# One gathered tile of 24 replaced by ScalarE column copies in a graph network layer

## The reference

```python
h = relu(layernorm(x))
m_in = concatenate([h[src], edge_attr], axis=1)
messages = relu(m_in @ msg_w1 + msg_b1) @ msg_w2 + msg_b2
aggregated = segment_sum(messages, dst, 12500)
u = relu(concatenate([h, aggregated], axis=1) @ upd_w1 + upd_b1)
out = x + u @ upd_w2 + upd_b2
```

## Time and profile before

| | us |
|---|---|
| median of 3 runs | 4632.11 |
| lowest to highest | 4628.16 to 4644.86 |
| the profiled execution | 4667.21 |
| its span in the trace | 4665.5 |

### The profile page before, as it was taken

One profiled execution on the slowest core, in us unless ns is written; L12 is line 12 of the kernel. 1 busy time (PEld: TensorE's weight loads), 2 busy tenths in 40 slices (PEclk: granted clock), 3 DMA queues, 4 the chain that ended last, 5 costly groups with the idle time before them and its releaser, 6 DMA issues.

```text
span 4665.5 us, 32266 instructions
## 1 busy us (share of the span) xinstructions
PE 2529.9 (54%) x10696; PEld 2174.4 (47%) x10696; DVE 1923.7 (41%) x1990; ACT 129.8 (3%) x257; POOL 2961.3 (63%) x3133
## 2 busy tenths in 40 slices
PE   5666555555555555555555555555555555535455
PEld 4555444444444444444444444444444444435344
DVE  4556343343343343443443443443433433434344
ACT  3310000000000000000000000000000000000000
POOL 5565666666666666666666666666666666656565
PEclk7777666676676666666666666666666666766666
DMA  5322222222222222222222222222222222233222
GB/s 146 103 84 71 67 66 72 67 66 72 67 70 68 66 71 67 67 71 67 67 71 66 67 71 66 67 71 66 66 72 66 66 72 67 80 88 88 83 78 59
DMA packets 154626, 340.79 MB, mean 73 GB/s; under 512 B 73895, under 2 KB 74919, under 8 KB 154187
## 3 DMA queue, kind: packets, MB, share of 16 engines
q0 software_dynamic: 100000, 205.00, 16.8%
q1 hardware_dynamic: 46165, 121.97, 8.1%
q10 hardware_dynamic: 8406, 13.14, 0.9%
HBM read 327.06 MB, written 12.81 MB: 73 GB/s over the span
## 4 chain that ended last, share of the span: by engine, by line
issue 40%; PE 38%; POOL 10%; another core or an unknown queue 5%; DVE 5%; DMA 1%; DVEq 0%; ACT 0%; ACTq 0%; POOLq 0%
PE pre L492 20%; PE seg L545 14%; POOL rows L405 10%; DVE rows L972 2%; DMA rows<-table,index 1%; DVE h_space L1026 1%; PE spare L560 1%; PE spare L561 1%; PE seg L463 1%; DVE space L1012 0%; PE pre L467 0%; PE pre L513 0%; PE spare L590 0%; PE pre L455 0%
## 5 line engine op out<-in xcount | busy, mean ns | idle before, releaser
L405 POOL DMA_INDIRECT rows<-table,index x3045 | 2884.4, 947 | 1621.7 <-issue 1100.7
L492 PE MATMUL pre<-w_attr_sb,attrs 128*128 128x256 f32 x3126 | 1334.6, 598 | 1331.5 <-issue 1194.2
L492 PEld LDWEIGHTS pre<-w_attr_sb,attrs 128*128 128x128 f32 x3126 | 905.9, 304 | 1593.8 <-issue 1272.7
L972 DVE TENSOR_TENSOR rows<-pre,rows 128x1024 f32<-128x1024 f32 x381 | 465.9, 1223 | 2301.0 <-DMA rows<-table,index 2207.7
L545 PE MATMUL seg<-space,rows 128*128 128x80 f32 x6250 | 973.7, 307 | 619.2 <-issue 617.0
L545 PEld LDWEIGHTS seg<-space,rows 128*128 128x128 f32 x6250 | 991.9, 232 | 649.5 <-issue 604.0
L1092 DVE TENSOR_TENSOR rows<-rows,iota_ps 128x1024 f32<-128x1024 f32 x381 | 464.8, 1220 | 13.1
L1026 DVE TENSOR_REDUCE h_space<-space 128x240 f32<-128x1920 f32 x130 | 438.4, 3372 | 0.0
L1012 DVE TENSOR_TENSOR space<-iota_ps,dst_rel 128x1920 f32<-128x1920 f32 x131 | 280.9, 2144 | 7.3 <-issue 5.9
L792 ACT ACTIVATE h_space<-update 128x500 f32<-128x500 f32 x25 | 27.6, 1104 | 4352.4 <-DVEq L1095 4181.3
L405 POOL DMA_INDIRECT rows<-in_x,index x80 | 75.8, 948 | 62.5 <-DVE rows L877 33.1
(11 more groups left out here) (77 smaller groups left out, 435.1 us busy)
## 6 DMA issues: line engine op xcount, KB each, us to landing
attrs<-in_attr SPq DMA_DIRECT2D x130, 768.0 KB
rows<-table,index POOLq DMA_INDIRECT x3045
table<-rows SPq DMA_DIRECT2D x20, 224.0 KB
h_space<-in_x ACTq DMA_DIRECT2D x13, 224.0 KB
out<-h_space ACTq DMA_DIRECT2D x13, 224.0 KB
table_first<-in_x ACTq DMA_DIRECT2D x12, 224.0 KB
out<-table_first ACTq DMA_DIRECT2D x12, 224.0 KB
x_all<-in_x SPq DMA_DIRECT2D x2, 1120.0 KB
```

Source lines behind the costliest of these rows:

```text
L405: pool.indirect_dma_start(slot_rows(j)[:, t, :], None, source, bass.IndirectOffsetOnAxis(index[0:EDGES, j, t:t + 1], 0))\
L492: return pe.matmul(columns(j, q, PAIR)[:, two * 2 * D:(two + 1) * 2 * D], attrs[:, j % 2, start:start + EDGES], w_attr_sb[:, :], start=Tru ...
L972: dve.tensor_tensor(hidden, columns(j, q, tiles), hidden, ALU.add).then_inc(summed, 1)
```

## The change

In the 106 blocks 8 to 113 (`COLS_FROM` to `COLS_END` - 1) GpSimd no longer gathers the last tile of chunk 2. SyncE loads the tile's 128 source indices (512 B, one partition) two blocks ahead into the space of `table_first`, behind each block's attribute load. ScalarE gets a loop, `take_columns`: for each block it waits for the indices and for the chunk 2 product of two blocks back, then four times loads 32 indices into registers and copies 32 columns of `h_all`, one instruction for each column, into a 128 x 128 buffer (`cols`, two of them, used in turn). TensorE's product of chunk 2 waits for the buffer and multiplies it with `w_src` on top of the attribute product of that tile. VectorE adds `b_msg1` to that tile by itself and adds gathered rows to seven tiles instead of eight. The counts of the `gathered` semaphores follow. `load_x(0)` and `load_x(1)` come after ScalarE's loop, since they use the same space. The gates of the early chunks and the leads are as before. Parts of the diff that only declare are left out.

```diff
 TILES_B = PAIRS * PAIR
 SLOTS = 8
 RING = 4
+COL_TILES = 1
 AHEAD = 5
 LEAD = 3
 FIRST_LEADS = {3: 12, 4: 12, 5: 12, 6: 12, 7: 12, 8: 12, 9: 10, 10: 7}
...
     PADDED = max(WINDOWS * WIDE, N - 1 + WINDOW)
     ROUNDS = BLOCKS // SLOTS - 2
     FINAL = ROUNDS * SLOTS
+    COLS_FROM = SLOTS
+    COLS_END = FINAL + 2
     DP = dst_rows.shape[0]
     DT = dst_rows.shape[1] // EDGES
 
...
         x_all = sb("x_all", [P, J * D])
         x_nodes = x_all[0:NP, :].rearrange("p (g r d) -> p g r d", g=GROUPS, r=ROWS)
         h_all = x_all[:, 0:N]
+        cols = [[x_all[:, N + n * EDGES:N + (n + 1) * EDGES], (identity, w_node_sb)[n][:, :]] for n in range(2)]
         update = sb("update", [P, PADDED])
 
         dst_rel = sb("dst_rel", [P, max(DT * EDGES, ALL_TILES)])
...
         h_early_t = h_space[:, 0:PAIR * P].rearrange("p (t e) -> p t e", t=PAIR)
         u = h_space[:, 0:ROWS * NP].rearrange("f (r p) -> f r p", r=ROWS)
         table_first = sb("table_first", [P, ROWS, D])
+        cols_index = table_first[0:1].rearrange("p r d -> p (r d)")[:, 0:2 * COL_TILES * EDGES].bitcast(I32)
         x_final = [h_space[0:NP, ROWS * D:2 * ROWS * D].rearrange("p (r d) -> p r d", r=ROWS), table_first[0:NP]]
         spot = 2 * ROWS * D
         base_row = h_space[0:1, spot:spot + (BLOCKS + 1) * BASES].bitcast(I32)
...
 
             return rows[0:EDGES, j % RING]
 
+        def has_cols(b, q):
+
+
+            return q == PAIRS - 1 and (not isinstance(b, int) or COLS_FROM <= b < COLS_END)
+
+        def gathered_tiles(b, q):
+
+            return tiles_of(b, q) - (COL_TILES if has_cols(b, q) else 0)
+
+        def gathered_by(i, b, q):
+
+
+            before = i * PAIR
+            if q == PAIRS - 1:
+                if not isinstance(b, int):
+                    before = i * (PAIR - COL_TILES) + COL_TILES
+                elif b >= COLS_FROM:
+                    before = i * PAIR - COL_TILES * len([n for n in range(b % SLOTS, b, SLOTS) if COLS_FROM <= n < COLS_END])
+            return 16 * (before + gathered_tiles(b, q))
+
         def h_group(g):
 
             return h_all[:, bass.ds(g * GROUP, GROUP)]
...
                     need(sp, summed, b * PAIRS + (PAIRS - (SLOTS - AHEAD) * PAIRS))
                     load_index(*nxt)
                 load_attr(i, j)
+                if not isinstance(b, int) or COLS_FROM <= b + 2 < COLS_END:
+                    if isinstance(b, int) and b + 2 == COLS_FROM:
+
+                        sp.wait_ge(table_stored[0], 16 * len(CUT) * GBODIES)
+
+                    need(sp, cols_made, b + (1 - COLS_FROM))
+                    width = COL_TILES * EDGES
+                    sp.dma_start(cols_index[:, j % 2 * width:(j % 2 + 1) * width], src_cols[bass.ds(b + 2, 1)]).then_inc(cols_index_loaded[j % 2], 16)
             for j in range(SLOTS):
                 load_block(0, j)
             with sp.Fori(1, ROUNDS) as i:
...
                     lead = FIRST_LEADS.get(b, LEAD) if isinstance(b, int) else LEAD
                     need(pool, hidden_summed, b * PAIRS + (q + 1 - lead))
                     pool.sem_inc(pool_turns, 1)
-                    gather(table, j, range(q * PAIR, q * PAIR + tiles_of(b, q)))
+                    gather(table, j, range(q * PAIR, q * PAIR + gathered_tiles(b, q)))
 
             pool.wait_ge(index_early_loaded, 16)
             for s in range(EARLY_CHUNKS):
...
                 if q == 0:
                     attr_loaded_for(i, j)
                 need(pe, summed, b * PAIRS + (q - 1))
-                for two in range(-(-tiles_of(b, q) // 2)):
-                    last = attr_product(i, j, q, two, True)
+                pairs = -(-tiles_of(b, q) // 2)
+                for two in range(pairs):
+                    last = attr_product(i, j, q, two, not (has_cols(b, q) and two == pairs - 1))
+                if has_cols(b, q):
+
+                    pe.wait_ge(cols_made, b + (1 - COLS_FROM))
+                    for c in range(COL_TILES):
+                        t = PAIR - COL_TILES + c
+                        last = pe.matmul(columns(j, q, PAIR)[:, t * D:(t + 1) * D], cols[j % 2][c], w_src_sb[:, :],
+                                         start=False, stop=c == COL_TILES - 1)
                 last.then_inc(pre_ready, 1)
 
             def early_products(j, q):
...
                     act.wait_ge(out_stored[(g - 1) % 2], 16 * len(CUT) * ((g - 1) // 2 + 1))
                     load_x(g + 1)
 
+            src_registers = [act.alloc_register(f"src{e}") for e in range(32)]
+
+            def take_columns(half, n):
+
+
+                act.wait_ge(cols_index_loaded[n], (half - (COLS_FROM // 2 - 1)) * 16)
+                act.sem_inc(act_turns, 1)
+                act.wait_ge(pre_ready, (half * 2 + n - 2) * PAIRS + PAIRS)
+                act.sem_inc(act_turns, 1)
+                for part_of in range(COL_TILES * EDGES // 32):
+                    start = n * COL_TILES * EDGES + part_of * 32
+                    act.load(src_registers, cols_index[0:1, start:start + 32])
+                    for e in range(32):
+                        node = bass.RuntimeValue.of_register_unchecked(src_registers[e], min_val=0, max_val=N - 1)
+                        c, column = divmod(part_of * 32 + e, EDGES)
+                        last = act.copy(cols[n][c][:, column:column + 1], h_all[:, bass.ds(node, 1)])
+                last.then_inc(cols_made, 1)
+
+            with act.Fori(COLS_FROM // 2, COLS_END // 2) as half:
+                for n in range(2):
+                    take_columns(half, n)
+
             act.wait_ge(table_stored[0], 16 * len(CUT) * GBODIES)
             load_x(0)
             load_x(1)
...
                                       b_msg1_bc[0:EDGES, :].unsqueeze(1).to_broadcast([EDGES, tiles, D]), ALU.add).then_inc(summed, 1)
                 else:
 
-                    dve.wait_ge(gathered[j][q], i * (16 * PAIR) + 16 * tiles)
-                    hidden = hidden.rearrange("p t d -> p (t d)")
+                    if has_cols(b, q):
+                        tiles -= COL_TILES
+                        dve.tensor_tensor(hidden[:, tiles:PAIR, :], columns(j, q, PAIR)[:, tiles * D:PAIR * D].rearrange("p (t d) -> p t d", t=COL_TILES),
+                                          b_msg1_bc[0:EDGES, :].unsqueeze(1).to_broadcast([EDGES, COL_TILES, D]), ALU.add)
+                    dve.wait_ge(gathered[j][q], gathered_by(i, b, q))
+                    hidden = hidden[:, 0:tiles, :].rearrange("p t d -> p (t d)")
                     dve.tensor_tensor(hidden, columns(j, q, tiles), hidden, ALU.add).then_inc(summed, 1)
 
             def early_statistics(s):
...
     arrays = {
         "x": x,
 
+        "src_cols": src[:body].reshape(blocks, TILES_B, EDGES)[:, TILES_B - COL_TILES:].reshape(blocks, COL_TILES * EDGES),
         "src": src[:body].reshape(blocks, TILES_B, EDGES).transpose(0, 2, 1), "src_last": src[body:].reshape(-1, EDGES).T,
         "dst_rows": filled(dst, P * depth * EDGES, n - 1).reshape(P, depth * EDGES),
         "dst_cols": filled(dst, tiles * EDGES, -1).reshape(tiles, EDGES).T,
```

More of the change, by code:

```diff
@@ L41, in after, with gnn_layer @@
     return step + (CREDIT + 1 - back)
-def gnn_layer(nc, x, src, src_last, dst_rows, dst_cols, attr, attr_last, w_src, w_attr, b_msg1, w_msg2_t, b_msg2, w_node, w_agg, b_upd1,
+def gnn_layer(nc, x, src, src_last, src_cols, dst_rows, dst_cols, attr, attr_last, w_src, w_attr, b_msg1, w_msg2_t, b_msg2, w_node, w_agg, b_upd1,
               w_upd2, b_upd2, out):
@@ L237, in gnn_layer @@
         updates_in = sem("updates_in")
+        cols_index_loaded = [sem(f"cols_index_loaded{n}") for n in range(2)]
+        cols_made = sem("cols_made")
         index_next_loaded = sem("index_next_loaded")
```

## The result

The changed kernel takes 4752.78 us (median; 4744.68 to 4758.09), the kernel before, run beside it, 4637.07 us: a ratio of 1.0246 (95% interval 1.0208 to 1.0285). It is slower, as forecast, but by 116 us, where 828 were forecast: it lies under the forecast's own range (5010 to 5745) and inside the whole range only because that reaches down to the faster case. The profiled execution took 4752.5 us, its span is 4750.7. The profiled execution of before lay 0.8% above its median, so between the two traces the difference is 85 us.

What follows compares the result with a forecast made beforehand. GpSimd's gather stream was taken to pace the kernel, 34.84 us a block; ScalarE's 106 sets of 42.3 us would end at 4849, the finish and rest bring 5500, by ratio 5460 us. Own range 5010 to 5745, whole range 4480 to 5745.

Steps and rivals of the forecast that it cites:

- the faster case: ScalarE's column loop fits into 33.6 us per block: 4505 us, or 4479 with the gap counted per gather; chance 0.28.
- the rival that counted the gap for each gather: GpSimd's 5.1 us gap is a price per gather, 1.45 us each: 154 us go, 4479 us; within the faster case, 0.28.
- The form of the sum: ScalarE's 106 sets in series from 365.4 end at 4849; block 112's finish, 12 us, and the rest, 637.4, follow.
- The 42.3 us per set: ScalarE's time per block: loads 25.4, copies 16.6, waits and semaphores 0.3 us; ends 10.0 and 60.9 us.
- the price of a load: ScalarE's load of 32 registers: 6.35 us, four per block 25.4 us, from 216 ns per further word on VectorE.
- The lower end: ScalarE's register loads: price hardly depends on length, 4 x 0.75 = 3.0 us per block, against 28.0 at the upper end.
- the faster rival: ScalarE's loads of up to 4.2 us each hide its whole list behind the gathers: 4505 us; chance 0.28.
- the gap of 5.1 us that the prediction took as given: GpSimd's gap after each block's 24 gathers, put down to the segment matmul L545; assumed to stay when one gather goes.
- a gap of 13 us at each block: Sign that the forecast is right: GpSimd's gap between blocks goes up from 5.1 to some 13 us.
- The last sign listed: ScalarE's copies alone taking over 0.2 us each would mean the sign holds and the reason is half right.
- The ratio of median to profiled execution: 0.9925, from median 4632.11 against 4667.2 us profiled; carried over, it turned the sum of 5500 into 5460 us.

Runs made afterwards that it cites:

- e3: Changed kernel, but ScalarE copies the first 128 columns with one instruction per block, without register loads or choice of columns; 4498.37 us, ratio 0.9693 to the kernel before.
- e2: Changed kernel with own registers for each of the eight loads of two blocks, so all are in the program; 5110.02 us, ratio 1.1005 to the kernel before.
- e5: Changed kernel with GpSimd gathering one tile of each chunk of eight instead of eight from block 8 on; 2201.1 us in one run.

## Why the prediction was right and wrong

**What bounds the kernel, and what a gather less gives**: right. Blocks take 33.30 us in e3; the whole saving was 1.54 us a block, more than the forecast's 1.25 and nearest to the rival that counted the gap for each gather, 1.45.

**The form of the sum**: right. First set at 362.15 (365.36 forecast); 106 sets in series end at 4099.1; block 112's finish and then block 113's product at 4123.95, 25 us later (12 forecast); the rest 626.8 us (637.4). 4099.1 + 24.9 + 626.8 = 4750.8, the span within rounding.

**The 42.3 us per set**: wrong, and with it 106 x 7.05 = 747 us of the sum. The step that failed is the price of a load, carried in a straight line from one and three words to 32. 1.95 us for 32 words (ScalarE) against 0.747 for three (VectorE) is 42 ns for each further word, not 216. The Trainium skill's "Runtime: NRT & Kernel Launch", section "Instruction fetch mechanics", had been weighed for the steep line (200 ns for each register, even in bulk); 1950 / 32 = 61 ns here, so it doesn't hold for this load, which comes from SBUF. The lower end, a price that hardly depends on length, was the nearer. Moreover only one load in eight was in the program that ran. Loads: 25.4 us forecast, 1.0 us (7.8 in e2). Copies: 0.13 us forecast, 0.093 measured back to back, 11.9 us a set.

**What was missing**: with these prices a set would be 13 us, in e2 some 20, and the faster rival would have come true: its condition, loads under 4.2 us, was met, and the time was not. What made the kernel slower is not in the forecast, which put this term at nothing: while GpSimd gathers, ScalarE's issue is held up, 22 us a set. So the sign was right by luck. It would have been luck too had the time fallen into the forecast's own range, as e2's did (5110 us, 38.6 us a set), the change as its source reads: its loads and copies are half of that, the hold-up is the rest. The trace of before had a sign of it, on TensorE; first a line of its waits from 490 to 3960 us, then of its timeline:

```profile
PE seg L545 <- issue: 507.5, 349, 2.6
...
2021.23 0.29 PE L545 MATMUL seg<-space,rows 128*128 128x80 f32 x1 [1.87 <-issue]
2023.32 0.29 PE L545 MATMUL seg<-space,rows 128*128 128x80 f32 x1 [1.80 <-issue]
2024.74 0.52 PE L545 MATMUL seg<-space,rows 128*128 128x80 f32 x2 [1.12 <-issue]
```

349 waits of TensorE for nothing that the profile shows, in the stage where ScalarE ran nothing, ask whether any instruction stream laid beside the gathers will pay the same. That question was not put. Over the whole span these waits are 617.0 us before and 9.9 us in e5, so they too go with the gathers. The three matmuls shown are the ones for which GpSimd stood in its gap to 2025.65: they too come in steps, and the last starts 4.1 us after the end of the last gather (2020.63). In the block shown, the gap of 5.1 us that the prediction took as given reads as the same hold-up, already paid by the kernel before. Also not counted as a rival was a built program that holds less than its source.

**What would show it**: TensorE's product waiting for the copies and the period equal to ScalarE's list came true; ScalarE at work to over 4800 us, loads of 6 to 7 us and a gap of 13 us at each block did not. The last sign listed, copies of over 0.2 us each, came in a way: less the loads a copy takes 0.27 us on average, but by the steps and not by its own length. The ratio of median to profiled execution, 0.9925 before, was 1.000 after; carrying it over was worth -41 us in the forecast.

## What to carry to other kernels

An engine that is idle in the profile is not a free place for a hundred tiny instructions beside a stream of gathers: count the instructions, and read the "issue" waits of the engines that already run beside it. Where only the two shortest lengths of a batched operation are in the trace, its price at a greater length is open between both ends (here 3.0 to 28.0 us a block), and a forecast that leans on one end rests on no row. The program as built should be compared with its source before its instructions are priced.

## What was not expected of the hardware

Beside GpSimd's indirect DMAs ScalarE's instructions, address instructions among them, come in steps of 0.7 and 1.4 us; the fast stretch (0.093 us a copy) follows GpSimd's gap by 3 to 4.5 us at most gaps. By the packet records of the changed kernel's trace the last gather's packets end 1.2 us after the gather, so the steps outlast both. Cutting the gathered bytes to an eighth changes a set from 35.25 to 34.4 us, cutting the gathers to one in eight makes it 12.0 us. Which part of a gather does it stays open, and so does whether the recording of the trace has a part in it.
